# Latents layer and closing layer of a two-layer decoder: two looped stages made into one unrolled pipeline of quads

## The reference

```
# fifth: latents. x is normed with g2, b2; the context with g1, b1
q  = ln_lat @ Wq                                  # 16 heads of 64
kv = concat([ln_ctx, ln_lat], axis=1) @ Wkv       # 128 keys a batch
weight = softmax(where(mask, (q * s) @ (k * s), -big))
y = (weight @ v) @ Wout
# sixth: closing layer, two quantised linear maps (128 -> 512 -> 128)
h = bitlinear(x, norm1_w, w1);  h = act_scale * relu(h)**2 + act_bias
y = bitlinear(h, norm2_w, w2)
# bitlinear: rms norm, scale by 127 / max|x| of the token, round, clip; ternary weights
```

## Time and profile before

| what | value |
|---|---|
| median of 3 runs | 2016.25 us (2013.1 to 2018.52) |
| the profiled execution: time | 2015.99 us |
| its span, first to last instruction | 2014.2 us |
| mean granted clock of PE in it | 0.877 of 2.4 GHz |
| PE / DVE / ACT / POOL busy | 1525.4 / 1358.7 / 829.6 / 361.7 us |

### The profile page before, as it was taken

One profiled execution on the slowest core, in us unless ns is written; L12 is line 12 of the kernel. 1 busy time (PEld: TensorE's weight loads), 2 busy tenths in 40 slices (PEclk: granted clock), 3 DMA queues, 4 the chain that ended last, 5 costly groups with the idle time before them and its releaser, 6 DMA issues. The chain is left out here.

```text
span 2014.2 us, 28424 instructions
## 1 busy us (share of the span) xinstructions
PE 1525.4 (76%) x10850; PEld 793.9 (39%) x10850; DVE 1358.7 (67%) x2359; ACT 829.6 (41%) x1141; POOL 361.7 (18%) x309
## 2 busy tenths in 40 slices
PE   5788767777778768888888738999999999983222
PEld 3555444454433323333333424444444444431111
DVE  3765655767555579888888617575675675466997
ACT  2222122322234358888888723332332332313444
POOL 2232212323200021111110013332322322120000
PEclk9889868887778879999999959999999999996555
DMA  3000000000000000000000010000000000000000
GB/s 135 1 1 2 1 11 12 6 12 6 1 0 0 0 1 1 1 1 1 1 1 1 1 53 6 6 5 0 5 5 0 5 0 0 0 0 0 11 10 21
DMA packets 14814, 16.46 MB, mean 8 GB/s; under 512 B 640, under 2 KB 13056, under 8 KB 14336
## 3 DMA queue, kind: packets, MB, share of 16 engines
q1 hardware_dynamic: 14432, 14.47, 2.1%
q10 hardware_dynamic: 288, 0.67, 0.1%
HBM read 13.04 MB, written 2.10 MB: 8 GB/s over the span
## 5 line engine op out<-in xcount | busy, mean ns | idle before, releaser
L1427 POOL PARTITION_BROADCAST l_share<-l_recip x128 | 103.9, 812 | 376.5 <-issue 207.0
L1283 ACT ACTIVATE l_prob<-psum,l_bias_now 128x1024 f32<-128x1024 f32 x64 | 71.3, 1114 | 221.3 <-PE psum L1191 221.3
L1349 DVE TENSOR_REDUCE l_top<-psum 128x8 bf16<-128x1024 f32 x64 | 77.3, 1207 | 126.2 <-PE psum L1177 124.5
L1216 PE MATMUL psum<-l_prob,l_X 128*128 128x512 f32 x256 | 124.9, 611 | 12.7 <-DVE l_px L1343 12.7
L1185 PE MATMUL psum<-l_th,l_XT 128*128 128x512 f32 x256 | 126.0, 615 | 7.2 <-ACT l_prob L1283 7.2
L1343 DVE TENSOR_TENSOR l_px<-psum,l_share 128x1024 f32<-128x1024 f32 x64 | 78.0, 1219 | 71.7 <-PE psum L1216 45.3
L1161 PE MATMUL psum<-l_XT,l_A 128*128 128x512 f32 x256 | 117.5, 604 | 9.3 <-ACT l_XT L1269 9.3
L1240 PE MATMUL psum<-l_px,l_N 128*128 128x512 f32 x256 | 111.5, 593 | 2.1 <-DVE l_px L1343 2.1
L1337 DVE CAST l_th<-l_th 128x512 bf16<-128x512 f32 x128 | 89.3, 739 | 29.2 <-ACT l_th L1272 29.2
L1356 DVE RECIPROCAL l_recip<-psum 128x512 f32<-128x512 f32 x32 | 107.1, 3347 | 0.7 <-PE psum L1206 0.6
L1272 ACT COPY l_th<-psum 128x512 f32<-128x512 f32 x128 | 74.2, 586 | 74.5 <-PE psum L1161 74.5
(11 more groups left out here) (301 smaller groups left out, 3309.2 us busy)
## 6 DMA issues: line engine op xcount, KB each, us to landing
early_weights<-in_weights SPq DMA_DIRECT2D x1, 2405.0 KB, 15.1
c_cs<-in_ctx SPq DMA_DIRECT2D x8, 256.0 KB, 2.8
l_mats<-in_l_mats SPq DMA_DIRECT2D x1, 2048.0 KB, 8.0
l_craw<-in_ctx SPq DMA_DIRECT2D x8, 256.0 KB, 2.8
out<-b_normed SPq DMA_DIRECT2D x8, 256.0 KB, 2.3
late_weights<-in_weights SPq DMA_DIRECT2D x1, 1089.0 KB, 11.0
relbias<-in_relbias ACTq DMA_DIRECT2D x1, 512.0 KB, 4.9
early_weights<-in_weights SPq DMA_DIRECT2D x1, 385.0 KB, 4.2
```

The costliest lines, as they stand in the source:

```text
L1216: last = nc.tensor.matmul(ps[:, 4 + q, :], X[:, b, :], prob[:, b % 4, q, :], start=True, stop=True)
L1349: nc.vector.tensor_reduce(top[:, b % 4, :], ps[:, 0:2, :].rearrange("p a (j n) -> p (a j) n", n=P), AX.X, ALU.max, negate=True).then_inc(s ...
L1427: nc.gpsimd.partition_broadcast(share[:, p % 2, n // 2, n % 2, :], recip[32 * n:32 * n + 1, p % 2, :], P).then_inc(s["share"], 1)
```

## The change

`latents_phase` and `bitlinear_phase` become one `latents_bitlinear_phase`. The groups become Q = 16 quads of QB = 4 batches (TQ = 2 tiles). Loops become one unrolled list of steps i from -9 to 89 on every engine. Step i works on batch i; `job(i, d)` gives the quad q whose work of delay d falls on the step (i = 4q + d), `chunk(i, d)` the quad and which quarter of it. Heads are made four at a time, one chunk a step, five steps ahead; combine likewise, six steps behind. Tokens and the hidden layer of the closing part follow their quad at delays 10 to 25. The weights of the closing layer are quantised in the block that folds the matrices. Moved between engines: the bf16 copy of `th` goes from DVE to POOL (`cast`), the product with `b_n2` from DVE to POOL (`normed_hidden`). Keys by token come by four DMAs a quad on SP's queue, from `cx` and `lat` to a threefold `X`. Copies of `stream` after norming are gone: norming is done in place. The moments of the fifth layer are used per quad, so the `norm_phase` and the barrier between the two are gone. The buffer `th` is now double, `XT` and `XT16` threefold.

```diff
+            def keys_in(q):                                   # SP
+                sp.wait_ge(s["staged"], q + 1)
+                if q >= 3:
+                    sp.wait_ge(s["px_ps"], QB * (q - 2))
+                for par in range(2):
+                    rows = slice(S * par, S * par + S)
+                    sp.dma_start(X[0:S, q % 3, par::2, :], cx[rows, :, :]).then_inc(s["X_in"], 16)
+                    sp.dma_start(X[S:P, q % 3, par::2, :], lat[rows, :, :]).then_inc(s["X_in"], 16)
...
             for i in range(FIRST, LAST):                      # PE
                 banks_free(i)
                 if 0 <= i < B:
                     scores(i)
                     shift(i)
                 q, k = chunk(i, -5)
                 if q is not None:
                     heads(q, k)
                 if job(i, 13) is not None:
                     pairs = min(max(0, (i - 2) // 2 + 1), B // 2)
                     pe.wait_ge(s["recip"], pairs)
                     tokens_turned(job(i, 13))
                 if 0 <= i - 2 < B:
                     gather(i - 2)
                 if i % 2 == 1 and 0 <= i < B:
...
                     sums((i - 1) // 2)
                 if 0 <= i < B:
                     pe.wait_ge(s["exped"], i + 1)
                 if job(i, -6) is not None:
                     columns_in(job(i, -6))
                 if job(i, 10) is not None:
                     turn_back(job(i, 10))
                 if job(i, 15) is not None:
                     hidden(job(i, 15))
                 if job(i, 21) is not None:
                     hidden_turned(job(i, 21))
                 if job(i, 22) is not None:
...
                     down(job(i, 22))
                 q, k = chunk(i, 6)
                 if q is not None:
                     combine(q, k)
                 if 0 <= i + 1 < B:
...
                     rough(i + 1)
...
+            def tokens_quantised(q):                          # DVE
+                if q >= 1:
+                    dve.wait_ge(s["x_ps"], q)
+                quantise(xn, xi, xscale, amax, roots[:, 1, :]).then_inc(s["x_ready"], 1)
+                if q >= 1:
+                    dve.wait_ge(s["r_sb"], TQ * q)
+                nc.vector.tensor_scalar(deq[:, :], amax[:, :], 1.0 / 127.0, wmean[:, 0:1], ALU.mult, ALU.mult).then_inc(s["deq1"], 1)
...
+            for i in range(FIRST, LAST):                      # DVE
+                if 0 <= i < B:
+                    row_tops(i)
+                if i % 2 == 0 and 0 <= i - 2 < B:
+                    invert((i - 2) // 2)
+                if job(i, 12) is not None:
+                    tokens(job(i, 12))
+                if job(i, 21) is not None:
+                    hidden_quantised(job(i, 21))
+                if 0 <= i - 2 < B:
+                    divide(i - 2)
+                if job(i, 12) is not None:
+                    tokens_quantised(job(i, 12))
+                if job(i, 17) is not None:
+                    scaled_hidden(job(i, 17))
+                if job(i, 25) is not None:
+                    normalise(job(i, 25))
+                if job(i, -9) is not None:
+                    prepare(job(i, -9))
+                if job(i, 19) is not None:
+                    hidden_biggest(job(i, 19))
+                if job(i, 10) is not None:
+                    residual(job(i, 10))
+                if job(i, 22) is not None:
+                    down_read(job(i, 22))
...
+            def cast(q, k):                                   # POOL
+                pool.wait_ge(s["th_sb"], QB * q + k + 1)
...
+                nc.gpsimd.tensor_copy(th16[:, q % 2, :, QB * k:QB * k + QB, :], th[:, q % 2, :, QB * k:QB * k + QB, :]).then_inc(s["th16"], 1)
+            def normed_hidden(q):
...
+                nc.gpsimd.tensor_tensor(hn[:, :, :], hh[:, :, :], w("b_n2").unsqueeze(1).to_broadcast([P, TQ, HID]), ALU.mult
+                                        ).then_inc(s["hn"], 1)
+            for i in range(FIRST, LAST):                      # POOL
+                if i % 2 == 0 and 0 <= i - 2 < B:
+                    spread((i - 2) // 2)
+                q, k = chunk(i, -5)
+                if q is not None:
+                    cast(q, k)
+                if job(i, -8) is not None:
+                    prepare(job(i, -8))
+                if job(i, 18) is not None:
+                    normed_hidden(job(i, 18))
```

More of the change, by code:

```diff
@@ L1144, in _ @@
+            context_in(0)
+            context_in(1)
+            for i in range(FIRST, LAST):
+                if job(i, -7) is not None:
+                    keys_in(job(i, -7))
+                if job(i, -16) is not None and job(i, -16) >= 2:
+                    context_in(job(i, -16))
+                if job(i, 25) is not None:
+                    store(job(i, 25))
+            for n in range(2):
+                sp.wait_ge(s[f"stored{n}"], 16 * Q // 2)
         @block.tensor
         def _(pe):
[L1146 to L1161, removed]
@@ L1181, in scores, with banks_free @@
[L1181 to L1191, removed]
+            def banks_free(i):
+                if job(i - 1, -6) is not None:
+                    pe.wait_ge(s["XT_sb"], job(i - 1, -6) + 1)
+                if job(i - 1, 10) is not None:
+                    pe.wait_ge(s["out_read"], job(i - 1, 10) + 1)
+                if job(i - 1, 15) is not None:
+                    pe.wait_ge(s["r_sb"], TQ * (job(i - 1, 15) + 1))
+                if job(i - 1, 21) is not None:
+                    pe.wait_ge(s["hiT_sb"], TQ * (job(i - 1, 21) + 1))
@@ L1210, in gather @@
[L1210 to L1213, removed]
-                    pe.wait_ge(s["px_sb"], Count(g, GB)(b))
-                for q in range(2):
-                    last = nc.tensor.matmul(ps[:, 4 + q, :], X[:, b, :], prob[:, b % 4, q, :], start=True, stop=True)
-                last.then_inc(s["px_ps"], 1)
-            def start(g):
-                keys_back(g)
-                rough(g, 0)
-                scores(g, 0)
-                rough(g, 1)
@@ L1225, in main @@
-            def main(g):
-                for b in range(GB):
-                    if b >= 1:
-                        scores(g, b)
-                    shift(g, b)
-                    if b + 2 < GB:
-                        rough(g, b + 2)
-                    if b >= LAG:
-                        gather(g, b - LAG)
-                    if b % 2 == 1:
-                        sums(g, b // 2)
-            def combine(g):
-                pe.wait_ge(s["px_sb"], Count(g, GB)(GB))
-                for h in range(H):
-                    last = nc.tensor.matmul(ps[:, 6, :], N[:, h, :], px[:, h, :, :], start=(h == 0), stop=(h == H - 1))
-                last.then_inc(s["y_ps"], 1)
@@ L1257, in _, with heads @@
-            main(G - 1)
-            for b in range(GB - LAG, GB):
-                gather(G - 1, b)
-            combine(G - 1)
-            finish(G - 1)
+            def heads(q, k):
+                if QB * q + k >= 1:
+                    pe.wait_ge(s["th_sb"], QB * q + k)
+                pe.wait_ge(s["XT_sb"], q + 1)
+                for j in range(QB):
+                    last = nc.tensor.matmul(ps[:, RO + j // 2, (j % 2) * 256:(j % 2 + 1) * 256], A[:, QB * k + j, :], XT[:, q % 3, :, 1, :],
+                                            start=True, stop=True)
+                last.then_inc(s["th_ps"], 1)
@@ new lines, in normalise @@
+            def normalise(q):
+                dve.wait_ge(s["root3"], q + 1)
+                step(nc.vector.reciprocal(std3[:, :], std3[:, :]))
+                if q >= 2:
+                    dve.wait_ge(s[f"stored{q % 2}"], 16 * (q // 2))
+                for t in range(TQ):
+                    last = nc.vector.tensor_scalar(normed[:, q % 2, t, :], z3[:, t, :], mom3[:, t, 0:1], std3[:, t:t + 1],
+                                                   ALU.subtract, ALU.mult)
+                last.then_inc(s["normed"], 1)
```

809 lines of the change are left out of this document (393 added, 416 removed).

## The result

The changed kernel takes 2120.09 us (median, 2118.85 to 2121.07), the kernel before 2017.38 measured beside it: a ratio of 1.051, 95% interval 1.048 to 1.053. It is slower, as forecast, but by 5.1% where 2.2% were forecast, and 5 us above the upper end of the range.

What follows compares the result with a forecast made beforehand. PE bounded the latents stage and DVE the closing layer; merged, DVE's order and waits for POOL would set the pace. Fill 1219, 64 batches 768 and drain 72 gave a 2059 span, 2061 us, 2.2% slower; range 1940 to 2115.

Steps and rivals of the forecast that it cites:

- first maxima: End of the fill: the first row maxima start at about 1219 us, 5 us before now.
- drain: Work remaining after the last of the 64 loop steps, including the store: 72 us.
- step 3: Loop step with remainder 3 modulo 4: divide waits for gather; 9.25 us by DVE, no meeting with POOL.
- steps 0 and 2: Loop steps by remainder modulo 4: divide waits for POOL's broadcasts, and port waits lengthen them to 14.6 and 14.0 us.
- price list of POOL: POOL's added work in the loop: cast 1.5 us, staging products 0.95 each, hn 1.9.
- the first broadcast starts 0.2 later: In two steps of each quad, POOL's first broadcast follows the inverted sums by 0.2 us; the second ends at 6.5.
- The steps that were too dear: Loop losses per quad: DVE's small operations waiting for POOL, 4.9 and 2.9 us, and PE's slow clock, 1.2.
- only wide operations are held: DVE's 2-column operations do not wait for POOL: 44 us a quad, 1997 us total; chance 0.18.
- The base: Sum of a quad's four loop steps with nothing lost to POOL: 39.0 us, 9.8 a batch.
- PE sets the pace: PE's work, not DVE's order, bounds the loop: 64 batches in 560 us, 1851 us total; chance 0.03.
- my 48.0 each: Loop time per quad including port waits and PE's clock: 48 us, 12.0 a batch.
- products are held too: DVE's small two-operand products also wait for POOL, three waits of 1.0: 53.1 us a quad, 2143 us; chance 0.06.

Runs made afterwards that it cites:

- experiment 7: Changed kernel, POOL broadcasting only, prepare and staging ahead of a divide on DVE, each quad's key DMAs issued twice: 1920.66 us, ratio 0.952 against 0.954 without.
- experiment 8: Kernel of experiment 5 with prepare and staging ahead of step 3's divide: 1923.28 us; then scaled_hidden and hn also moved later, ahead of the preceding divide: 1945.27 us.
- experiment 6: Changed kernel with staging products and hn done by no engine and the bf16 copy of th on ACT: 1921.44 us, ratio 0.953.
- experiment 5: Changed kernel with staging products and hn on DVE and the bf16 copy of th on ACT, leaving POOL broadcasts alone: 1957.93 us, ratio 0.972.
- experiment 1: Changed kernel plus an 8-column POOL broadcast right behind the staging products and behind hn, so POOL changes early: 2041.14 us, ratio 1.011.

## Why the prediction was wrong in size

**What held.** Slower; first maxima at 1217 (1219); drain 75.8 (72); removed stages gone; keys by DMA hidden (experiment 7); ACT hidden; DVE's order sets step 3 and not its sum (experiment 8); maxima 14 or more apart in steps 0 and 2; some small operations of DVE far above 0.2 us; granted clock below 1.00 (0.87). One sign failed beside the size: POOL's staging did not stand directly behind its cast and under quantise, but 7.4 us later.

**The step that failed** is the price list of POOL, "POOL gets the bf16 cast of th (four per quad), hn, and seven staging products of half the size". It priced the instructions (cast 1.04 us for my 1.5, product 0.71 for 0.95, hn 2.35 for 1.9) and not the changes between them. With it fell the sentence "the first broadcast starts 0.2 later", which carried rows 8, taken inside a group, to a kernel that changes kind in each step of that sort. The missing term is 6.0 us for each change to broadcasts, twice a quad once hn runs (from step 18) and once before and near the end: 26 changes in the run, of which 25 lie in the 826 us of the loop, some 150 us (an estimate: 25 times the mean delay). The trace of before had it, with 207 us of "issue" at seven broadcasts.

**The steps that were too dear** hid part of it. Against experiment 6, the changed kernel's steps are longer by 6.5, 1.6, 6.6 and 1.0, 15.7 a quad. I had forecast 9.0 of such loss (4.9 and 2.9 held by POOL, 1.2 of clock). 12.0 of the 15.7 are the late broadcasts and 1.3 the casts (experiment 5); 2.4 are left for the products' holds and PE's slow starts together. The trace says where these fall. In step 1 the heads, behind the long pause, take 3.5 us in the mean and not 1.95, ahead of the gather that divide waits for. In step 3, where I had forecast nothing, prepare runs beside hn and the cast, and its four norming operations take 2.5 to 3.1 us where they take 1.36 in experiment 6. A second slow start, of the scores at the end of step 2 (3.75 us for 1.94), is hidden, as the next shift waits for the row maxima even so. The hold itself is real, and on small operations too. DVE's groups by line in the changed kernel:

```profile
L1583 DVE TENSOR_SCALAR l_normed<-l_z,l_mom,l_std 128x128 f32<-128x128 f32 x32 | 22.8, 754 | 0.6
...
L1514 DVE TENSOR_SCALAR l_xscale<-l_xscale 128x2 f32<-128x2 f32 x16 | 10.8, 678 | 0.5
...
L1511 DVE TENSOR_TENSOR l_amax<-l_amax,l_roots 128x2 f32<-128x2 f32 x16 | 8.3, 517 | 0.1
...
L1514 DVE TENSOR_SCALAR l_hscale<-l_hscale 128x2 f32<-128x2 f32 x16 | 2.7, 170 | 0.5
...
L1511 DVE TENSOR_TENSOR l_amax<-l_amax,l_ss 128x2 f32<-128x2 f32 x16 | 2.6, 160 | 0.6
```

L1514 is the same operation twice: 170 ns where POOL is quiet (hscale), 678 under the cast (xscale); in the timeline above it takes 0.98 and ends with the cast. So the rival "only wide operations are held" falls. In the sum over all groups of like work DVE's durations are 42 us longer than in the kernel of experiment 5, 2.6 a quad instead of 7.8. The reason is the change itself: POOL's products start 7.4 us behind the cast, when quantising is over, and meet normalise behind the divide of step 1. What that costs is mostly slack, since the row maxima behind it wait for PE's rough (0.32 us even so at 1635.96). hn too comes 7 us late and so meets prepare in step 3. The one mis-forecast moved most of the other out of the way.

**The base** of 39.0 a quad is 41.1 (experiment 6): step 1 is 1.0 and step 0 0.6 longer than summed. Why was not looked into. The working has two slips besides: the terms given for step 0 (0.7, 1.2 and four of 0.8) add up to 5.1 and not 4.9, and the rival "PE sets the pace" leaves out the 2 us around the span.

**By quads**, against my 48.0 each: the first four took 168.9 us, 23 less, since the closing layer asks little of them yet, which I had left out; the fifth 3 more; the eight in the middle 456.5, 72 more; the last three 150.0, 6 more. That is the 58 us between 768 and 826. The forecast was thus as near as it was in part by luck: the term left out, some 150 us, was offset by holds priced too high and by the cheap first quads.

**The rival "products are held too"** gave 2143, 23 us from the result, but not by its cause: a product of 128x2 takes 517 ns beside broadcasts and 160 without (L1511 twice), 0.36 us a quad, where I had put three waits of 1.0 and a full clock loss. So such products are held, by far less.

**Open** is how the 2.4 us a quad divide between holds and PE's clock, why the base was short in steps 0 and 1, and what POOL does during a change.

## What to carry to other kernels

Before moving an operation onto POOL, list POOL's instructions in their new order and count the changes between broadcasts and two-tensor products: 5.6 to 7.5 us each here, for operations of 8 to 1024 columns. Avoid them (copies and casts needed none here), or put the change ahead of the wait, which gave back 79 us here, where moving all products gave 150. An idle time that a profile puts down to "issue" is a price; find the cheapest row that has it, and ask how often the new order pays it. When the path is cured, the order of an in-order engine is next: 35 us came from moving one job ahead of a wait. But ask first what ends the next wait: the second such move cost 22 us.

## What the hardware showed that was not expected

- A change of kind on POOL takes 5.6 to 6.0 us to broadcasts and 6.7 to 7.5 to products in the changed kernel. It starts only when the waits ahead of the first instruction of the new kind are over (configuration at 1611.8, reciprocal's end at 1611.3). A product of 8 columns in each pair costs 172 us; a copy nothing.
- POOL with a busy share of 24% set the pace of a loop to within about 1 us (experiment 1).
- The configuration in the profile is not itself the price: from a product of two tensors to operations with a scalar it stands there too, and these start 0.1 us later.
- Contention beside a broadcast runs both ways: a broadcast of 0.80 us took 1.40 beside a DVE product of 1024 columns, which took 1.56 for 1.23.
